# A two-layer transformer block on one core: layer 1's threshold flag a section earlier, transposed chunks in pairs, the output share split over ScalarE and GpSimd, and 128-row row scores in layer 0

## Chip, cores, metric

One NeuronCore of a Trainium2 chip. The time is device microseconds of the whole program for one launch; lower is better. Everything is in one kernel: two layers, each with attention and a feed-forward part.

## What is computed

```python
x = L0_attn_x                                   # (2, 1024, 128) float32
xn = layernorm(x)
x = x + attn0(xn) + moe(xn)                     # attn0: 16 heads of 8, causal softmax; moe: 8 experts, top 2
xn = layernorm(x)
x = x + attn1(xn) + trees(xn)                   # trees: 8 binary trees of depth 7
# attn1: 16 query heads of 64 over 4 key/value heads, rotary positions
scores = where(future, -1e30, q @ k.T / 8)      # 1024 x 1024 for each batch and head
threshold = top_k(scores, 64)[-1]               # the 64th largest of each row
weights = softmax(where(scores < threshold, -1e30, scores))
out = (weights @ v) @ Wo.T
```

## The kernel before

The program runs stage after stage: projections, attention of layer 0, experts, projections of layer 1, trees, attention of layer 1. Each stage writes one instruction list for each engine by hand; semaphores join them. The change touches the two attention stages. B x H heads make 32 in each layer; a sequence of 1024 is 8 row tiles of 128 (`TB = 8`).

**Layer 0** (`attend_layer0`, tensors `a0_`; the profile prints them as `a_`). A section of the loop `heads` works on head n and on the rows of head n+1. TensorE scores head n+1 row by row in 12 units of up to 512 columns (`row_unit`, L350, and for a diagonal tile the mask, L353), VectorE takes each unit's maxima (`peaks`, L463) and from them makes the shift of each row. The queries and keys for this use are 64 partitions (`SHIFT0`) high. The shift is turned (L394) and copied by ScalarE into partitions 64 to 66 of `q` (L439). Then the scores are made again, column by column over 128 partitions (L407, mask L410), so that the shift comes out of the same product; ScalarE exponentiates them (L445), and the product with v follows in three parts `pv` (L374, 32 columns of the array). ScalarE copies the result out (L451) after the sixth column tile; TensorE turns it back (L424); `keep` on VectorE divides. `rows_ahead` puts the row units between the column tiles: 2, then 2, 1, 2, 1, 1, 1, 1, 1. GpSimd only copies v (L331), once in a section.

**Layer 1** (`attend_layer1`). A section n of the loop `sections` has four heads in work: VectorE copies the scores of head n+1 out of PSUM (`keep_scores`, L1463, eight row tiles); ScalarE counts for head n how many scores lie above a trial value (`count`, L1332, eight tiles, three rounds c = 0, 1, 2; VectorE's `first_move` and `second_move`, L1526 to L1581, make the next trial from each round); VectorE sorts head n-1: `tally` (L1421) and `split_tally` read the three rounds, `mark` (L1436) keeps what lies below the value found, `sort` takes 8 + 8 largest in three passes (L1448, L1450, L1452), and the tail to L1693 makes threshold and verdict. Tiles 7 and 6 (1024 and 896 columns) are marked by GpSimd with a compare and a multiply (L1307, L1312, number `EARLY = 2`). Head n-2 is finished: TensorE sums the verdict over the partitions (L1260), VectorE reads that flag (`flags`, L1470), loads it to a register and branches (`judge`: an exact search in the rare bad case), `cut_off` (L1502) writes the cutoffs, ScalarE makes the gates `short` (`gate`, L1342), TensorE turns scores and gates together (`turn`, L1224 and L1226, up to 4 tiles in a chunk, 12 chunks), ScalarE exponentiates a chunk (`weights`, L1351), and TensorE multiplies it with v (`weigh`, L1237). `turn` of chunk x+2 stands behind `weigh` of chunk x. Head n-3 leaves: `copy_out` (L1358), `project` (L1249, eight products of 129 columns, the last of them the softmax sum), and on VectorE `shares` (L1510, the reciprocal) and `leave` (L1519, `x += projected * rec`, from PSUM).

All lists are in program order. TensorE begins a section with the flag of head n-2:

```python
pe.wait_ge(verdict_ready, n - 1)
wait(pe, t_read, (n - 2) * TU)
pe.matmul(ps_flag, g.ones[:, 0:1], verdict[:, :], start=True, stop=True).then_inc(flag_back, 1)
```

ScalarE's section is: counts of round 0, gates of tiles 7 to 4, round 1 with `weights` 0 to 3 between the counts, gates 3 to 0 and `weights` 4, round 2 with `weights` 5 to 8, `weights` 9 to 11. VectorE's is: tally, flag, the first two score copies, judge and cutoff, shares and six sums into x, then marks, score copies and sorting passes, with the steps of the two moves between them.

## Time and profile before

| | |
|---|---|
| median of 3 runs | 2691.27 us (2687.34 to 2691.73) |
| the profiled execution | 2691.92 us, its span 2689.9 us |
| TensorE busy | 2060.2 us, 77% of the span |
| VectorE busy | 1710.9 us, 64% |
| ScalarE busy | 1415.4 us, 53% |
| GpSimd busy | 393.6 us, 15% |
| layer 0's attention | about 110 to 545 us of the span |
| layer 1's attention | about 1210 us to the end |

Busy shares are means over stages with different limits, and a busy TensorE is not one at its peak, since its rows overlap. In a row of the timeline stand the start, the duration and, in brackets, the idle time of that engine before it with what ended it. Neighbouring rows of VectorE and ScalarE overlap by some 0.1 us. Where the kernel repeats a section, one of them is enough: from a section's first row to the next one's.

### The profile page before, as it was taken

What the parts mean: (1) busy time and instruction counts of PE and PEld (TensorE: products, weight loads), DVE (VectorE), ACT (ScalarE), POOL (GpSimd) and SP (SyncE); (2) the same over time, 40 slices, a digit from 0 to 9 for tenths busy, and PEclk for the clock granted to TensorE, in tenths of its full rate; (3) what the DMA queues carried; (4) which work ended last, traced back from release to release, by engine and by line L of the source; (5) the groups of instructions that cost most, each with busy time, mean ns of one, the idle gap of its engine ahead of it and who ended that gap; (6) DMA issues with size and microseconds to landing.
All of it is one profiled execution on the core that took longest, in us unless ns stands there. A gap on an engine that the chain in (4) does not pass through costs nothing. (4 is left out here: it accounts for less than half of the span.)

```text
span 2689.9 us, 36464 instructions
## 1 busy us (share of the span) xinstructions
PE 2060.2 (77%) x10416; PEld 1158.8 (43%) x10448; DVE 1710.9 (64%) x4622; ACT 1415.4 (53%) x2979; POOL 393.6 (15%) x262
## 2 busy tenths in 40 slices
PE   6799999899988968885676777777767567767766
PEld 4233333377764435552343444444434334434434
DVE  4556656521125666765886777777777777877784
ACT  2344444444324213324766666666666566766673
POOL 0000000000012400001212121222212212221211
PEclk7699999999968969997788878788888778888877
DMA  6000000000011200001000000000000000000000
GB/s 179 18 16 15 15 15 15 8 28 1 0 39 55 88 15 0 0 5 44 21 13 25 13 25 12 25 12 24 14 24 17 20 12 18 19 24 12 17 5 21
DMA packets 38267, 62.43 MB, mean 23 GB/s; under 512 B 10226, under 2 KB 15348, under 8 KB 38005
## 3 DMA queue, kind: packets, MB, share of 16 engines
q1 hardware_dynamic: 38069, 60.51, 7.7%
q14 instruction: 161, 1.31, 0.2%
q8 instruction: 37, 0.61, 0.1%
HBM read 34.14 MB, written 17.83 MB: 19 GB/s over the span
## 5 line engine op out<-in xcount | busy, mean ns | idle before, releaser
L1332 ACT ACTIVATE a_trash<-a_sc,a_search 128x1024 bf16<-128x1024 f32 (+7 forms) x768 | 585.7, 766 | 294.2 <-DVE a_search L1581 164.4
L1237 PE MATMUL a_ps_o<-a_kT,a_v 128*65 128x512 f32 (+3 forms) x768 | 376.8, 584 | 214.8 <-ACT a_kT L1351 213.6
L1208 PE MATMUL a_ps_s<-a_k,a_q 128*128 128x512 f32 (+3 forms) x768 | 343.5, 562 | 141.5 <-DVE a_sc L1463 128.1
L1307 POOL TENSOR_SCALAR a_below<-a_sc,a_found 128x1024 f32<-128x1024 f32 x64 | 171.9, 2686 | 1103.5 <-POOLq L1303 1103.5
L1224 PE MATMUL a_ps_t<-g_ident,a_sc 128*128 128x128 f32 x1152 | 298.2, 331 | 33.4 <-ACT a_short L1342 33.3
L463 DVE TENSOR_REDUCE a_top<-a_ps_row 128x1 f32<-128x512 f32 (+3 forms) x384 | 207.4, 557 | 161.4 <-PE a_ps_row L353 107.6
L1226 PE MATMUL a_ps_t<-a_minus,a_short 128*128 128x128 bf16 x1152 | 268.0, 253 | 0.0
L1224 PEld LDWEIGHTS a_ps_t<-g_ident,a_sc 128*128 128x128 f32 x1152 | 199.2, 173 | 154.9 <-issue 92.0
L1351 ACT ACTIVATE a_kT<-a_ps_t 128x512 f32<-128x512 f32 (+3 forms) x384 | 184.6, 481 | 118.8 <-PE a_ps_t L1226 115.0
L1208 PEld LDWEIGHTS a_ps_s<-a_k,a_q 128*128 128x128 f32 x768 | 142.2, 214 | 235.9 <-DVE a_sc L1463 140.5
L445 ACT ACTIVATE a_prob<-a_ps_col 128x1024 f32<-128x1024 f32 (+7 forms) x256 | 158.3, 653 | 147.2 <-PE a_ps_col L407 113.0
L1342 ACT ACTIVATE a_short<-a_sc,a_cutoff 128x1024 bf16<-128x1024 f32 (+7 forms) x256 | 177.0, 764 | 95.3 <-DVE a_cutoff L1502 95.1
L1463 DVE TENSOR_SCALAR_CACHE_REDUCE a_sc<-a_ps_s,g_search 128x1024 f32<-128x1024 f32 (+7 forms) x256 | 207.2, 809 | 24.6 <-PE a_ps_s L1210 9.0
L1237 PEld LDWEIGHTS a_ps_o<-a_kT,a_v 128*65 128x65 f32 x768 | 88.7, 158 | 285.6 <-ACT a_kT L1351 238.0
L1448 DVE MAX8 a_sorted<-a_below 128x8 f32<-128x768 f32 (+7 forms) x256 | 192.8, 754 | 1.2
L1452 DVE MAX8 a_sorted<-a_below 128x8 f32<-128x768 f32 (+7 forms) x256 | 192.5, 752 | 0.0
L1450 DVE MATCH_REPLACE8 a_below<-a_sorted,a_below 128x768 f32<-128x768 f32 (+7 forms) x256 | 189.5, 742 | 0.0
L1226 PEld LDWEIGHTS a_ps_t<-a_minus,a_short 128*128 128x128 bf16 x1152 | 139.8, 121 | 91.6 <-issue 91.5
L584 ACT ACTIVATE ex_hid<-ex_ps_h,le_b 128x512 f32<-128x512 f32 x128 | 87.8, 687 | 128.5 <-PE ex_ps_h L561 128.1
L1332 ACT ACTIVATION_READ_ACCUMULATOR a_trash<-a_sc,a_search 128x1 f32 x768 | 147.0, 191 | 0.0
L350 PE MATMUL a_ps_row<-a_k,a_q 64*128 64x512 bf16 (+3 forms) x384 | 132.5, 346 | 13.9 <-DMA a_k<-stack 12.7
L1312 POOL TENSOR_TENSOR a_below<-a_sc,a_below 128x1024 f32<-128x1024 f32 x64 | 142.4, 2225 | 2.8
(244 smaller groups left out, 3218.3 us busy)
## 6 DMA issues: line engine op xcount, KB each, us to landing
a_v<-g_v SPq DMA_DIRECT2D x32, 260.0 KB, 2.3
q1turned<-p_full SPq DMA_DIRECT2D x32, 256.0 KB, 2.0
a_q<-q1turned SPq DMA_DIRECT2D x32, 256.0 KB, 3.6
a_k<-k1turned SPq DMA_DIRECT2D x32, 256.0 KB, 4.1
stack<-p_parts SPq DMA_DIRECT2D x24, 256.0 KB, 3.8
a_q<-stack SPq DMA_DIRECT2D x32, 96.0 KB, 2.2
a_k<-stack SPq DMA_DIRECT2D x32, 96.0 KB, 2.2
le_w<-d_w SPq DMA_DIRECT2D x1, 2048.0 KB, 8.9
```

The lines of the kernel that those rows point to most:

```text
L463: m = dve.tensor_reduce(top[:, i, c:c + 1], ps_row[:, u % 2, 0:width], AX.X, ALU.max)
L1208: pe.matmul(ps_s[:, j % 2, c:c + w], q[:, p, i * P:width], k[:, p, c:c + w], start=True, stop=True)
L1224: pe.matmul(out, columns(h, i)[:, c * P:(c + 1) * P], g.ident[:, :], is_transpose=True, start=True, stop=False)
L1226: m = pe.matmul(out, short[:, OFF[i] + c * P:OFF[i] + (c + 1) * P], minus[:, :], start=False, stop=True)
L1237: m = pe.matmul(ps_o[0:VW1, lo // HALF, (lo % HALF) * P:CH], v[:, p, c, :], kT[:, x % 2, 0:(hi - lo) * P], start=(c == 0), stop=(c == hi - 1))
L1332: act.activation(trash[:, u % 2, 0:(i + 1) * P], columns(h, i), ACT.Sign, scale=-1.0, bias=trials[:, p, c, i:i + 1], accum_out=balance[:, ...
L1342: act.activation(short[:, OFF[i]:OFF[i] + (i + 1) * P], columns(h, i), ACT.Relu, scale=-STEEP, bias=cutoff[:, h % 2, i:i + 1]).then_inc(ga ...
L1351: act.activation(kT[:, x % 2, 0:w], ps_t[:, x % 2, 0:w], ACT.Exp).then_inc(t_read, 1)
L1448: m = dve.max(sorted_[:, i, 0:8], buf)
L1450: m = dve.match_replace(buf, sorted_[:, i, 0:8], buf, -3.0e38)
L1452: m = dve.max(sorted_[:, i, 8:16], buf)
L1463: dve.tensor_scalar(columns(h + 1, i), ps_s[:, j % 2, 0:(i + 1) * P], shift.rearrange("p n i -> p (n i)"), None, ALU.subtract, ALU.max, ac ...
```

## The change

Layer 0: the row scores use all 128 partitions of `q` and `k`. Partitions 64 to 66 of `q` must then be zero, so GpSimd clears them (`clear`, a sum of two zero tiles) once the head that used them is done, and TensorE waits on `cleared` before a head's first row unit. The row units go 2, 2, 2, 2, 2, 2 between the column tiles. Layer 1: `EARLY` is 3, so GpSimd marks tile 5 too; 12 chunks become 9, each of four tiles; the flag's matmul moves from the head of a section to the chunk loop of the section before, ahead of the last `weigh`; VectorE's list gets a new order; VectorE keeps only the reciprocals of a leaving head, ScalarE scales the eight projected tiles into `share`, and GpSimd adds them to `x` in three pieces. Output transfers wait for those sums.

```diff
-                pool.wait_ge(blank, 3)
+                def clear(n, h):
+
+                    pool.wait_ge(v_ready, n + 2)
+                    pool.wait_ge(col_ready, n * CU + CU)
+                    pool.tensor_tensor(q[SHIFT0:SHIFT0 + NSH, h, :], none[SHIFT0:SHIFT0 + NSH, :],
+                                       none[SHIFT0:SHIFT0 + NSH, :], ALU.add).then_inc(cleared, 1)
+                    pool.wait_ge(cleared, n + 1)
+
+                pool.wait_ge(blank, 4)
                 values(0, 0, True)
                 values(1, 1, True)
-                with pool.Fori(1, NH // 2) as i:
-                    values(i * 2, 0)
-                    values(i * 2 + 1, 1)
+                clear(0, 0)
+                values(2, 0)
+                clear(1, 1)
+                values(3, 1)
+                with pool.Fori(1, NH // NQ) as i:
+                    for h in range(NQ):
+                        clear(i * NQ + (h - 2), (h + 2) % NQ)
+                        values(i * NQ + h, h % 2)
...
                     if u == 0:
                         pe.wait_ge(qk_in[h], i4 * 32 + 32)
+                        wait(pe, cleared, i4 * NQ + (h - NQ + 1))
                     wait(pe, row_read, unit - 1)
-                    last = pe.matmul(ps_row[:, u % 2, 0:width], q[0:SHIFT0, h, i * P:(i + 1) * P],
-                                     k[0:SHIFT0, h, c * CH:c * CH + width], start=True, stop=True)
+                    last = pe.matmul(ps_row[:, u % 2, 0:width], q[:, h, i * P:(i + 1) * P],
+                                     k[:, h, c * CH:c * CH + width], start=True, stop=True)
...
-                        rows_ahead(2 if j in (0, 2) else 1)
+                        rows_ahead(2)
```

Layer 1, the constants, TensorE's loop, GpSimd and ScalarE:

```diff
-        EARLY = 2
+        EARLY = 3
...
-        CHUNKS = [(c, max(c, lo), lo + HALF) for lo in (HALF, 0) for c in range(lo + HALF)]
+        CHUNKS = ([((0, 0, 4),), ((1, 1, 4), (3, 3, 4))] + [((c, HALF, TB),) for c in range(5)]
+                  + [((5, 5, 8), (7, 7, 8)), ((6, 6, 8), (2, 2, 4))])
+        NARROW = 2
+        LAST = (2, 6)
+        GATES = [0, 1, 2, 3, 7, 6, 5, 4]
...
-                def turn(n, h, x):
-
-                    c, lo, hi = CHUNKS[x]
+                def turn(n, h, u, x):
+
                     if x == 0:
                         pe.wait_ge(gated, n * TB + HALF)
-                    if x == EARLY_CHUNKS:
+                    if x == NARROW:
                         pe.wait_ge(gated, n * TB + TB)
...
-                    if gating:
-                        pe.wait_ge(verdict_ready, n - 1)
-                        wait(pe, t_read, (n - 2) * TU)
-                        pe.matmul(ps_flag, g.ones[:, 0:1], verdict[:, :], start=True, stop=True).then_inc(flag_back, 1)
...
+                    odd = h % 2
                     if gating:
-                        turn(n - 2, h + 2, 0)
-                        turn(n - 2, h + 2, 1)
+                        turn(n - 2, h + 2, odd, 0)
+                        turn(n - 2, h + 2, odd + 1, 1)
                     for x in range(TU):
+                        if sorting and x == TU - 1:
+                            pe.wait_ge(verdict_ready, n)
+                            pe.matmul(ps_t[0:1, 1 - odd, 0:TB + 1], g.ones[:, 0:1], verdict[:, :], start=True,
+                                      stop=True).then_inc(flag_back, 1)
                         if gating:
-                            weigh(n - 2, i4 * 2 + h // 2 - 1, h % 2, x)
+                            weigh(n - 2, i4 * 2 + h // 2 - 1, h % 2, odd + x, x)
                             if x + 2 < TU:
-                                turn(n - 2, h + 2, x + 2)
-                        if ahead and x < HALF:
-                            scores(n + 1, i2, p1, HALF + x)
-                        if late and x in (9, 11):
-                            scores(n + 2, i4 * 2 + (h + 2) // 2, 1 - p1, x // 2 - 4)
+                                turn(n - 2, h + 2, odd + x, x + 2)
+                        if ahead and x in (0, 1, 3, 5):
+                            scores(n + 1, i2, p1, HALF + (x + 1) // 2)
+                        if late and x in (6, 7):
+                            scores(n + 2, i4 * 2 + (h + 2) // 2, 1 - p1, x - 6)
...
+                def add(n, x):
+                    lo, hi = ((0, 3), (3, 6), (6, 8))[x]
+                    out = g.x.rearrange("p (b t) d -> p b (t d)", b=B)
+                    xs = out[:, bass.ds(n // H1, 1), lo * P:hi * P].rearrange("p b d -> p (b d)")
+                    pool.wait_ge(shared, n * TB + hi)
+                    pool.tensor_tensor(xs, xs, share[:, lo * P:hi * P], ALU.add).then_inc(added, 1)
...
+                def leave(n, x):
+
+                    lo, hi = ((0, 3), (3, 6), (6, 8))[x]
+                    act.wait_ge(rec_ready, n * 3 + (x + 1))
+                    for t in range(lo, hi):
+                        if t == 0:
+                            wait(act, added, n * 3)
+                        bank, a = PROJ[t]
+                        act.activation(share[:, t * P:(t + 1) * P], projected[bank][:, a, 0:P], ACT.Copy,
+                                       scale=rec[:, t:t + 1]).then_inc(shared, 1)
...
+                    odd = h % 2
                     for s in range(TB):
                         if counting:
                             count(n, h, 0, s)
-                        if leaving and s == 1:
+                        if leaving and s == 2:
                             copy_out(n - 3)
+                    if leaving:
+                        leave(n - 3, 0)
+                        leave(n - 3, 1)
                     if gating:
                         for j in range(HALF):
+                            gate(n - 2, h + 2, j)
+                    if leaving:
+                        leave(n - 3, 2)
+                    if gating:
+                        for j in range(HALF, TB):
                             gate(n - 2, h + 2, j)
                     for s in range(TB):
                         if counting:
                             count(n, h, 1, s)
                         if gating and s % 2:
-                            weights(n - 2, s // 2)
+                            weights(n - 2, odd + s // 2, s // 2)
                     if gating:
-                        for j in range(HALF, TB):
-                            gate(n - 2, h + 2, j)
-                        weights(n - 2, HALF)
+                        weights(n - 2, odd + HALF, HALF)
                     for s in range(TB):
                         if counting:
                             count(n, h, 2, s)
                         if gating and s % 2:
-                            weights(n - 2, HALF + 1 + s // 2)
-                    if gating:
-                        for x in range(2 * HALF + 1, TU):
-                            weights(n - 2, x)
+                            weights(n - 2, odd + HALF + 1 + s // 2, HALF + 1 + s // 2)
```

VectorE (what follows `shares(2)` is the same kind of work in another order; `mark(5)` and `leave` are gone):

```diff
-                        after(did(dve.reciprocal(rec[:, lo:hi], projected[PROJ[lo][0]][:, 0:hi - lo, P])))
-
-                    def leave(x):
-
-                        lo, hi = ((0, 3), (3, 6), (6, 8))[x]
-                        out = g.x.rearrange("p (b t) d -> p b (t d)", b=B)
-                        for t in range(lo, hi):
-                            bank, a = PROJ[t]
-                            xs = out[:, bass.ds((n - 3) // H1, 1), t * P:(t + 1) * P].rearrange("p b d -> p (b d)")
-                            dve.scalar_tensor_tensor(xs, projected[bank][:, a, 0:P], rec[:, t:t + 1], xs, ALU.mult,
-                                                     ALU.add).then_inc(x_kept, 1)
+                        if x == 0:
+                            wait(dve, shared, (n - 3) * TB)
+                        dve.reciprocal(rec[:, lo:hi], projected[PROJ[lo][0]][:, 0:hi - lo, P]).then_inc(rec_ready, 1)
...
                     if sorting:
                         tally()
                         split_tally()
-                    if gating:
-                        flagged = flags()
                     if ahead:
                         keep_scores(0)
                         keep_scores(1)
+                    if sorting:
+                        mark(4)
+                    if gating:
+                        flagged = flags()
+                    if sorting:
+                        mark(3)
                     if gating:
                         judge(flagged)
                         after(made[0])
                         cut_off()
+                    next(first, None)
+                    if sorting:
+                        mark(2)
+                    next(first, None)
                     if leaving:
                         shares(0)
+                    next(first, None)
+                    if leaving:
                         shares(1)
-                        leave(0)
-                        leave(1)
-                    if sorting:
-                        mark(5)
-                    next(first, None)
+                    for _ in first:
+                        pass
                     if ahead:
                         keep_scores(2)
-                    next(first, None)
                     if sorting:
-                        mark(4)
-                    next(first, None)
-                    if sorting:
-                        mark(3)
-                    next(first, None)
-                    if leaving:
-                        shares(2)
-                        leave(2)
-                    if sorting:
-                        mark(2)
-                        sort(5, 0)
                         mark(1)
                         sort(4, 0)
                         mark(0)
-                    for _ in first:
-                        pass
-                    if sorting:
-                        sort(5, 1)
+                        sort(3, 0)
                         sort(4, 1)
+                        sort(3, 1)
+                    if leaving:
+                        shares(2)
                     if ahead:
```

How this moves the instructions is shown at three places. In these rows `a_below` is what is marked and sorted, `a_sc` the scores, `a_rec` the reciprocal, `a_short` the gates; the last number is the columns of what is written.

VectorE at the head of a section, before:

```order
L1430 TENSOR_REDUCE a_found<-a_far 128x8
L1470 TENSOR_SCALAR a_flag<-a_ps_t 1x1
L1463 TENSOR_SCALAR a_sc,a_peak<-a_ps_s,g_search 128x1024
L1463 TENSOR_SCALAR a_sc,a_peak<-a_ps_s,g_search 128x896
L1490 TENSOR_LOAD a_flag
L1490 ISA x2
L1491 COMPARE_AND_BRANCH
```

and now, from the same instruction:

```order
L1479 TENSOR_REDUCE a_found<-a_far 128x8
L1512 TENSOR_SCALAR a_sc,a_peak<-a_ps_s,g_search 128x1024
L1512 TENSOR_SCALAR a_sc,a_peak<-a_ps_s,g_search 128x896
L1485 SCALAR_TENSOR_TENSOR a_below<-a_sc,a_found 128x640
L1519 TENSOR_SCALAR a_flag<-a_ps_t 1x1
L1485 SCALAR_TENSOR_TENSOR a_below<-a_sc,a_found 128x512
L1539 TENSOR_LOAD a_flag
L1539 ISA x2
L1540 COMPARE_AND_BRANCH
```

The flag is read after both score copies and one mark, another mark stands ahead of its load, and the branch follows.

VectorE from the cutoff on, before:

```order
L1502 SCALAR_TENSOR_TENSOR a_cutoff<-a_thr,a_ceiling 128x8
L1510 RECIPROCAL a_rec<-a_ps_o 128x3 x2
L1519 SCALAR_TENSOR_TENSOR g_x<-a_ps_o,a_rec,g_x 128x128 x6
L1436 SCALAR_TENSOR_TENSOR a_below<-a_sc,a_found 128x768
L1526 TENSOR_TENSOR a_reach<-a_wide_aim,a_balance 128x8
L1463 TENSOR_SCALAR a_sc,a_peak<-a_ps_s,g_search 128x768
L1542 RECIPROCAL a_fac<-a_reach 128x8
L1436 SCALAR_TENSOR_TENSOR a_below<-a_sc,a_found 128x640
L1545 TENSOR_TENSOR a_fac<-a_fac,a_search 128x8
L1436 SCALAR_TENSOR_TENSOR a_below<-a_sc,a_found 128x512
L1548 SCALAR_TENSOR_TENSOR a_search<-a_fac,a_search 128x8
L1510 RECIPROCAL a_rec<-a_ps_o 128x2
```

and now, from the first trial's last step to the third reciprocal, which stands eight rows further down:

```order
L1594 TENSOR_TENSOR a_gap<-a_search 128x8
L1512 TENSOR_SCALAR a_sc,a_peak<-a_ps_s,g_search 128x768
L1485 SCALAR_TENSOR_TENSOR a_below<-a_sc,a_found 128x256
L1497 MAX a_sorted<-a_below 128x8
L1485 SCALAR_TENSOR_TENSOR a_below<-a_sc,a_found 128x128
L1497 MAX a_sorted<-a_below 128x8
L1499 MATCH_REPLACE a_below<-a_sorted,a_below 128x640
L1499 MATCH_REPLACE a_below<-a_sorted,a_below 128x512
L1561 RECIPROCAL a_rec<-a_ps_o 128x2
```

Between cutoff and third reciprocal stand now the marks of tiles 2, 1 and 0 and four sorting passes; the sums into `x` are gone.

ScalarE from the end of round 0 on, before:

```order
L1332 ACTIVATE a_trash,a_balance<-a_sc,a_search 128x128
L1342 ACTIVATE a_short<-a_sc,a_cutoff 128x1024
L1342 ACTIVATE a_short<-a_sc,a_cutoff 128x896
L1342 ACTIVATE a_short<-a_sc,a_cutoff 128x768
L1342 ACTIVATE a_short<-a_sc,a_cutoff 128x640
L1332 ACTIVATE a_trash,a_balance<-a_sc,a_search 128x1024
L1332 ACTIVATE a_trash,a_balance<-a_sc,a_search 128x896
L1351 ACTIVATE a_kT<-a_ps_t 128x512
```

and now:

```order
L1368 ACTIVATE a_trash,a_balance<-a_sc,a_search 128x128
L1402 ACTIVATE a_share<-a_ps_o,a_rec 128x128 x6
L1378 ACTIVATE a_short<-a_sc,a_cutoff 128x128
L1378 ACTIVATE a_short<-a_sc,a_cutoff 128x256
L1378 ACTIVATE a_short<-a_sc,a_cutoff 128x384
L1378 ACTIVATE a_short<-a_sc,a_cutoff 128x512
L1402 ACTIVATE a_share<-a_ps_o,a_rec 128x128 x2
L1378 ACTIVATE a_short<-a_sc,a_cutoff 128x1024
L1378 ACTIVATE a_short<-a_sc,a_cutoff 128x896
L1378 ACTIVATE a_short<-a_sc,a_cutoff 128x768
L1378 ACTIVATE a_short<-a_sc,a_cutoff 128x640
L1368 ACTIVATE a_trash,a_balance<-a_sc,a_search 128x1024
```

All eight gates stand ahead of round 1, and two groups of `a_share` stand ahead of them and between them.

## Rows read from the trace of the kernel before

**Rows 1.** Busy time by stretch: span, PE, PEld, DVE, ACT, POOL, PEclk, DMA, GB/s.

```profile
130.00:534.00 404.00, 364.53 (x2437) 145.90 (x2459) 235.08 (x607) 199.80 (x297) 7.32 (x29) 0.99 0.05 13
...
1367.00:2075.00 708.00, 503.39 (x2334) 292.08 (x2333) 535.15 (x1566) 479.37 (x1119) 158.29 (x80) 0.84 0.07 19
```

**Rows 2.** Waits in sixteen sections of layer 1, 1367 to 2075 us: sum, times, longest.

```profile
DVE a_flag L1470 <- PE a_ps_t L1260: 90.6, 16, 7.3
...
DVE a_cutoff L1502 <- issue: 38.5, 16, 2.6
...
ACT a_trash L1332 <- DVE a_search L1581: 84.1, 16, 5.5
...
DVE a_above L1421 <- remote: 9.0, 3, 3.1
```

**Rows 3.** The instructions of L1421 between 1360 and 2080 us.

```profile
L1421 DVE TENSOR_TENSOR a_above<-a_wide,a_balance x17: 182/184/184, 1367.4 to 2078.8; 128x24 f32<-128x24 f32 x17
```

**Rows 4.** Timeline of TensorE in layer 0: start, duration, engine, line.

```profile
308.50 0.22 PE L407 MATMUL a_ps_col<-a_q,a_k 128*128 128x128 bf16 x1
308.65 0.28 PE L350 MATMUL a_ps_row<-a_k,a_q 64*128 64x256 bf16 x1
308.86 0.23 PE L353 MATMUL a_ps_row<-g_maskq,g_identb 128*128 128x128 bf16 x1
308.93 0.38 PE L407 MATMUL a_ps_col<-a_q,a_k 128*128 128x512 bf16 x1
```

**Rows 5.** Timeline of layer 0: TensorE, ScalarE, GpSimd, one section's end.

```profile
300.99 0.61 PE L394 MATMUL a_ps_col<-g_identb,a_shift 128*3 128x128 bf16 x8 [0.48 <-DVE a_shift L472]
...
312.68 1.37 PE L424 MATMUL a_ps_row<-g_ident,a_oT 128*128 128x128 f32 x8
...
311.40 1.02 ACT L451 ACTIVATE a_oT<-a_ps_out 128x1024 f32<-128x1024 f32 x1
...
310.88 0.25 POOL L331 COPY a_v<-l_v 128x72 f32 x1 [13.29 <-PE a_ps_out L374]
```

**Rows 6.** Timeline of VectorE and GpSimd at the head of a section of layer 1.

```profile
1723.41 0.18 DVE L1421 TENSOR_TENSOR a_above<-a_wide,a_balance 128x24 f32<-128x24 f32 x1 [2.96 <-remote]
...
1730.67 1.15 DVE L1463 TENSOR_SCALAR_CACHE_REDUCE a_sc<-a_ps_s,g_search 128x896 f32<-128x896 f32 x1 [0.27 <-DVE a_sc L1463]
...
1734.26 0.36 DVE L1502 SCALAR_TENSOR_TENSOR a_cutoff<-a_thr,a_ceiling 128x8 f32<-128x8 f32 x1 [2.43 <-issue]
...
1727.57 2.36 POOL L1312 TENSOR_TENSOR a_below<-a_sc,a_below 128x1024 f32<-128x1024 f32 x1
```

**Rows 7.** Timeline of GpSimd and VectorE where both read SBUF, an early section.

```profile
1297.07 2.08 POOL L1312 TENSOR_TENSOR a_below<-a_sc,a_below 128x896 f32<-128x896 f32 x1
...
1297.48 2.34 DVE L1436 SCALAR_TENSOR_TENSOR a_below<-a_sc,a_found 128x640 f32<-128x640 f32 x1
...
1260.76 2.51 POOL L1307 TENSOR_SCALAR a_below<-a_sc,a_found 128x896 f32<-128x896 f32 x1
...
1261.77 0.83 DVE L1436 SCALAR_TENSOR_TENSOR a_below<-a_sc,a_found 128x640 f32<-128x640 f32 x1
```

**Rows 8.** Timeline of ScalarE in layer 1: gates, and round 1 of the counts.

```profile
1734.74 3.62 ACT L1342 ACTIVATE a_short<-a_sc,a_cutoff 128x1024 bf16<-128x1024 f32 x4
...
1741.00 1.15 ACT L1332 ACTIVATE a_trash<-a_sc,a_search 128x1024 bf16<-128x1024 f32 x1 [2.64 <-DVE a_search L1548]
...
1748.42 0.20 ACT L1332 ACTIVATION_READ_ACCUMULATOR a_trash<-a_sc,a_search 128x1 f32 x1
```

**Rows 9.** Timeline of VectorE in layer 1: second move, first and last row.

```profile
1708.72 0.17 DVE L1526 TENSOR_TENSOR a_reach<-a_wide_aim,a_balance 128x8 f32<-128x8 f32 x1
...
1712.66 0.16 DVE L1581 SCALAR_TENSOR_TENSOR a_search<-a_fac,a_search 128x8 f32<-128x8 f32 x1
```

**Rows 10.** Timeline of TensorE in layer 1: one product with v, and a later one.

```profile
1743.80 1.97 PE L1237 MATMUL a_ps_o<-a_kT,a_v 128*65 128x512 f32 x2 [2.50 <-ACT a_kT L1351]
...
1750.33 1.02 PE L1237 MATMUL a_ps_o<-a_kT,a_v 128*65 128x512 f32 x2
```

101 lines of the change are left out of this document (54 added, 47 removed).

## The prediction

> **What bounds the kernel now.** I read the busy table by stretch first, then the waits of layer 1, then one section of each attention stage on every engine it uses. The span is 2689.9 us and the execution 2691.9, so 2.0 us lie around the span; the median of the runs, 2691.27, is 0.6 below this execution. The sum is made against 2691.9.
>
> Layer 0: TensorE is busy for 364.5 of 404 us at a granted clock of 0.99, that is at 2.4 GHz, and no other engine for more than 235 [rows 1]. It bounds that stage. A section lasts 13.54 us: GpSimd's copy of v, once in a section, was idle for 13.29 and ran for 0.25 [rows 5].
>
> Layer 1: nothing is full; in 708 us TensorE is busy for 503, VectorE for 535, ScalarE for 479 [rows 1]. Seventeen starts of L1421 lie from 1367.4 to 2078.8, so a section lasts 711.4 / 16 = 44.46 us [rows 3]. VectorE works without a gap except at a section's head: it waits 90.6 / 16 = 5.7 us for the flag and 38.5 / 16 = 2.4 us for the jump over the exact search. ScalarE waits 84.1 / 16 = 5.3 us for the second move [rows 2]. So VectorE's list, with 8 us of holes in it, sets the length, and ScalarE's last counts end just in time. The question for layer 1 is which chain is longest once the holes are filled.
>
> **The change in layer 0.** A product of 128 rows and 128 columns hands over to the mask's in 0.06 us or so: the 128-column mask to the next column product took 308.93 - 308.86 = 0.07. But the 128-row product of 128 columns at 308.50 took until 308.65 before the 64-row one began, 0.15, and that one took 0.21 for its 256 columns before the 128-row mask [rows 4]. At 0.07 for 128 columns they would take 0.07 and 0.12. Every change between 64 and 128 rows costs about 0.09 to 0.1 us. With 12 units in and out that is 24 changes, 2.3 us of a section. The Trainium skill, TensorEngine Tiling (Array Packing), speaks on both sides. Its Overview recommends a smaller tile for a contraction of up to 64, for up to twice the speed: by that the change could only lose; but a single tile is in use here at a time, and a 512-column product takes its columns' time at either height. Its Key Properties say that a change of tiling mode drains the engine; by that, the trace agrees.
>
> Not all of it reaches the end. TensorE waits at the head for ScalarE's copy of the shift, which the first two row units used to cover: 0.4 back. Three more row units now stand ahead of the last `pv` part (2+2+2+2+2+2 against 2+2+1+2+1+1 up to there), about 0.25 each, 0.75 back. So `pv` ends 2.3 x 9/12 less 0.4 and 0.75, only about 0.6 sooner counted from L394; the three units that used to fill TensorE's wait for the output copy are gone from there. L394 began at 300.99, the copy ended at 311.40 + 1.02 = 312.42 and the turns L424 followed at 312.68 for 1.37 [rows 5]: now the turns begin about 0.8 sooner, at 10.9 instead of 11.7, and since the rows are read earlier the 0.48 wait for the shift before L394 goes too. That is 1.25 a section; a stall on the two row buffers may take 0.15. I take 1.1 x 31 = 34 us. Bounds: 0.5 x 31 = 15 if VectorE's maxima hold the pairs up, 2.3 x 31 = 71 if no copy shows. GpSimd's clears lie two sections ahead of their use and cost nothing; without that lead TensorE would wait some 2.4 us for each, the time of its 1024-column product [rows 6].
>
> **The change in layer 1.** I follow one section from L1421 = 0, by the old section from 1723.41 on.
> - Head of VectorE. Tally and two score copies end at about 4.0 (keep_scores(1) was 1.15 [rows 6]), mark(4) at 4.75 (0.83 less overlap [rows 7]). The flag is there by then: verdict, matmul and return need about 3. The 5.7 us hole is gone. The jump stays: from keep_scores(1) to the cutoff were 1734.26 - 1730.67 = 3.6 us, and in it the sequencer, not the engine, is held; so the cutoff comes 3.6 after the flag at 4.85, at 8.4 instead of 10.85.
> - GpSimd in the way. An early section shows a mark of 640 columns that took 2.34 instead of 0.83 us: it began 0.41 after GpSimd's multiply and ended 0.67 after it, so it was held for 1.5 us. A mark of 640 beside GpSimd's compare ran in 0.83 [rows 7]. So a VectorE instruction with two SBUF inputs waits for the rest of a multiply, not of a compare. In the old section the marks came after GpSimd was done; now they stand inside its work, which EARLY = 3 lengthens. GpSimd began its multiply of 1024 at 1727.57, 4.2 in the section's time, for 2.36 [rows 6]. It now starts behind mark(4), 4.75 to 7.1; compare 896 (2.51) to 9.7; multiply 896 (2.08) to 11.8; compare and multiply of 768, by the same slope 2.2 and 1.8, to 14.0 and 15.9. Mark(3) is held until 7.1, hidden under the jump. The reciprocals 0 and 1 and `fac` come at about 9.7: held 2.0. Mark(0) at 14.7: held 1.2. With the passes between them (some 3,500 columns at 0.83 for 640, less overlap, 4.3 us) the third reciprocal is ready at 18.6; without the holds at 15.4.
> - ScalarE. Its `leave(2)` waits for that reciprocal, in front of four large gates and of round 1. Two scaled copies of 128 columns: 0.6, unknown, bounded by 0.3 and 0.8. Gates 3.6 [rows 8], so round 1 starts at 22.8. It takes 1748.62 - 1741.00 = 7.6 us [rows 8]: 30.4. In the old section it began at 17.6.
> - Second move: 1712.66 - 1708.72 = 3.9 before [rows 9], with shorter passes in it now 3.6: 34.1. VectorE is ahead and waits here, about 2.5 us.
> - Round 2 is like round 1, since all chunks are now 512 wide: 7.6, to 41.8. The next tally waits for it. VectorE's remaining passes end near 40.4.
> - TensorE's late score tiles stand behind `keep_scores(6)` and `(7)` and come about 0.4 late for the next head: 42.2. The loop's jump, 9.0 / 3 = 3.0 us in every fourth section [rows 2], was part of 44.46; VectorE now has 1.4 of slack for it, so it adds 0.4 on average: 42.6.
>
> So 44.46 - 42.6 = 1.9 us a section. Of the removed work (sums into x, 1.7 us or so for six, mark(5) 0.9) and the holes, over 8 us, most goes to a chain that runs through ScalarE. Over 29 full sections: 54 us. The first and last sections, where some parts are missing, and the end, where ScalarE and GpSimd replace one VectorE step by three, I leave at nothing, plus or minus 4. Fewer chunks save ScalarE nothing to speak of, since the elements are the same. **Sum:** 2691.9 - 34 - 54 = 2604.
>
> **Rivals.**
> (1) The holds do not happen, because GpSimd's multiplies fall between VectorE's two-input instructions. The reciprocal comes 3.2 sooner: 29 x 3.2 = 93 us less, 2511. For it: only two holds are counted. Against: both are longer than the gaps.
> (2) TensorE's chunk chain eats the gain. After a wait of 2.50 us a pair of products took 1.97 us, six us later 1.02, that is at 1.2 and at 2.4 GHz [rows 10]; now TensorE stands still for some 7 us before round 1. If `weights(4)` or the weights in round 2 come 1.9 late, layer 1 gains nothing: 2658.
> (3) Slower: the same mechanism in full. If TensorE stays at 1.2 GHz from the first product to the last, `weights(4)` ends 3.2 us late in front of round 2, and the chain through `weights(7)` ends the section at 48.7: 29 x 4.2 = 123 more, less 34: 2781. It decides from a section of 44.46 + 34/29 = 45.6 on.
> (4) GpSimd's compares hold VectorE too. Then the cutoff waits 1.2 for compare 896 and a mark up to 2.2 for compare 768: section 46.0, 2691.9 + 45 - 34 = 2703. The mark that ran in 0.83 beside a compare speaks against it [rows 7]. The Trainium skill, SBUF — State Buffer, Who interferes with whom, states it this way: a VectorE instruction with two SBUF inputs contends with any GpSimd instruction that reads SBUF. By that rule the time would be this 2703; the trace agrees for the multiply and not for the compare [rows 7].
> (5) The price of 64 rows is not the change of height, and the row units cost what they did: only 54 gained, 2638.
>
> **How the numbers follow.** Chances: forecast 0.45; (1) 0.20; (2) 0.20; (3) 0.05; (4) 0.04; (5) 0.06. A difference under 0.2%, 5 us, can't be told from none. The forecast, (1), (2) and (5) are faster, 0.91; the slower cases make 0.09, of which their near edges give 0.02 to "same". The range reaches from (1) to beyond (2): 2505 to 2668. Its own spreads leave about 8 in 10 inside.
>
> **What would show it.** Right: layer 0's copies of v about 12.4 us apart and no gap beyond 0.1 us between row unit and mask; no wait before the flag's read; two-input rows of VectorE of 1 to 2 us beside multiplies of GpSimd; ScalarE waiting before the third `a_share` group and starting round 1 near 23; VectorE waiting for round 1. Wrong: a section of L1421 to L1421 outside 41.5 to 43.7, VectorE never waiting for ScalarE, or a clock in layer 1 clearly off 0.84.

## The result, and the profile after

The changed kernel takes 2878.44 us, the median of 4 runs (2874.84 to 2879.5), against 2691.45 us for the kernel before, measured beside it. The ratio is 1.0696, with a 95% interval of 1.0678 to 1.0715. I forecast 2604, in a range of 2505 to 2668. The side is wrong, and the time lies 210 us above the range.

The engines first. The busy table by stretch for the kernel after gives layer 0, then about fourteen sections of layer 1 (columns as in [rows 1]):

```profile
130.00:496.00 366.00, 296.77 (x2314) 130.06 (x2316) 221.82 (x582) 188.83 (x277) 58.89 (x55) 1.00 0.05 14
...
1300.00:2010.00 710.00, 446.66 (x1996) 255.80 (x1995) 490.55 (x1218) 435.72 (x1036) 242.41 (x140) 0.74 0.06 17
```

In layer 1 every engine but GpSimd is less busy than in [rows 1]: VectorE 490.6 of 710 us against 535.2 of 708. No engine has become the bound; they wait for each other. The granted clock is 0.74 instead of 0.84; TensorE also stands still more of the time.

The first instruction of a section (L1421 before, L1470 now) over layer 1 of the kernel after:

```profile
L1470 DVE TENSOR_TENSOR a_above<-a_wide,a_balance x29: 182/184/185, 1305.1 to 2769.2; 128x24 f32<-128x24 f32 x29
```

That is 1464.1 / 28 = 52.3 us a section; one of them, 75.7 us long, holds the exact search, as one of 67.5 us does in the kernel before. An ordinary section is 51.27, and one with the loop's jump 54.2. Over all 32 starts layer 1 took 1366.4 us before and 1578.5 now, 212.1 more. Layer 0's copies of v are 13.18 us apart instead of 13.54, and layer 1 starts 26.1 us sooner. 212 - 26 = 186 of the 187 us are there: layer 1 alone is what has to be explained.

The waits of layer 1 in the kernel after, 1300 to 2800 us (in us: sum, times, longest):

```profile
DVE a_sc L1512 <- PE a_ps_s L1230: 329.6, 60, 7.4
PE a_ps_o L1261 <- ACT a_kT L1385: 318.8, 57, 9.1
...
ACT a_share L1402 <- DVE a_rec L1561: 272.4, 60, 30.3
...
ACT a_trash L1368 <- DVE a_search L1622: 120.0, 29, 4.4
...
DVE a_cutoff L1551 <- issue: 54.3, 22, 4.1
```

The first row has no counterpart in the same view of the kernel before. VectorE's copy of scores out of PSUM waits for TensorE's mask product 60 times, 329.6 / 29 = 11.4 us in a section. The wait for the flag, 5.7 us a section in [rows 2], is gone from the list.

One section on three engines, starting with L1470 at 1820.64. VectorE (start, duration; in brackets its idle time before):

```profile
1824.74 3.10 DVE L1485 SCALAR_TENSOR_TENSOR a_below<-a_sc,a_found 128x640 f32<-128x640 f32 x1
...
1831.53 0.87 DVE L1551 SCALAR_TENSOR_TENSOR a_cutoff<-a_thr,a_ceiling 128x8 f32<-128x8 f32 x1 [2.27 <-issue]
...
1839.82 0.17 DVE L1561 RECIPROCAL a_rec<-a_ps_o 128x2 f32<-128x2 f32 x1
...
1852.18 0.75 DVE L1512 TENSOR_SCALAR_CACHE_REDUCE a_sc<-a_ps_s,g_search 128x512 f32<-128x512 f32 x1 [7.20 <-PE a_ps_s L1230]
...
1860.61 0.15 DVE L1622 SCALAR_TENSOR_TENSOR a_search<-a_fac,a_search 128x8 f32<-128x8 f32 x1
...
1867.73 0.35 DVE L1512 TENSOR_SCALAR_CACHE_REDUCE a_sc<-a_ps_s,g_search 128x128 f32<-128x128 f32 x1 [4.53 <-PE a_ps_s L1230]
```

TensorE in the same section:

```profile
1846.84 1.97 PE L1261 MATMUL a_ps_o<-a_kT,a_v 128*65 128x512 f32 x2 [6.41 <-ACT a_kT L1385]
1851.70 0.31 PE L1230 MATMUL a_ps_s<-a_maskq,g_identb 128*128 128x128 bf16 x1
...
1863.67 1.97 PE L1261 MATMUL a_ps_o<-a_kT,a_v 128*65 128x512 f32 x2 [4.09 <-ACT a_kT L1385]
1867.24 0.31 PE L1230 MATMUL a_ps_s<-a_maskq,g_identb 128*128 128x128 bf16 x1
```

ScalarE in the same section:

```profile
1834.03 1.66 ACT L1402 ACTIVATE a_share<-a_ps_o,a_rec 128x128 f32<-128x128 f32 x6 [5.75 <-DVE a_rec L1561]
...
1840.02 0.62 ACT L1402 ACTIVATE a_share<-a_ps_o,a_rec 128x128 f32<-128x128 f32 x2 [2.54 <-DVE a_rec L1561]
1840.54 3.62 ACT L1378 ACTIVATE a_short<-a_sc,a_cutoff 128x1024 bf16<-128x1024 f32 x4
1844.05 1.14 ACT L1368 ACTIVATE a_trash<-a_sc,a_search 128x1024 bf16<-128x1024 f32 x1
...
1860.87 1.15 ACT L1368 ACTIVATE a_trash<-a_sc,a_search 128x1024 bf16<-128x1024 f32 x1 [4.28 <-DVE a_search L1622]
```

The three views read as one chain. ScalarE waits for VectorE's third reciprocal, starts round 1 at 1844.05 (23.4 into the section), and makes the first `weights` inside it. TensorE has stood 6.4 us for that, runs `weigh(0)` and the next turns, and only then scores tile 4, whose mask is at 1851.70. VectorE, out of work since 1844.98, copies it at 1852.18. Everything behind it on VectorE is late, the second move among it, so round 2 starts at 1860.87 (40.2). There the same happens again: `weigh(5)` needs a `weights` of round 2, tile 7 stands behind `weigh(5)`, and VectorE waits 4.53 us for tile 7 and then has its tail to do.

So the theory for the tests is **A**: score tiles 4 and 7 stand in TensorE's list behind products that wait for ScalarE, whose rounds wait for VectorE, and these two loops of waits make the section long. The rival **B**: VectorE's stalls beside GpSimd, ScalarE's longer list and TensorE's lower clock make it long, and the waits for score tiles are only where it shows.

### The profile page after: what moved, and what is told of

Its sections match the earlier page's. It is cut to its first block, busy times and chain, and to the rows that moved or that the text cites. A ratio compares the mean times of both kernels' runs of the same rounds, so it can differ in the third digit from the quotient of the medians.

```text
span 2876.7 us, 36532 instructions
## 1 busy us (share of the span) xinstructions
PE 2019.7 (70%) x10448; PEld 1154.7 (40%) x10448; DVE 1758.3 (61%) x4335; ACT 1468.8 (51%) x3139; POOL 687.5 (24%) x452
## 4 chain that ended last, share of the span: by engine, by line
DVE 22%; PE 13%; issue 11%; ACT 10%; DVEq 1%; SPq 0%; ACTq 0%; DMA 0%; POOL 0%; POOLq 0%
ACT a_short L1378 5%; PE a_ps_o L1261 5%; DVE a_below L1485 5%; DVE a_sc L1512 4%; DVE a_below L1499 3%; PE a_ps_t L1245 3%; ACT a_trash L1368 3%; PE a_ps_s L1228 3%; DVE a_sorted L1497 2%; PE a_ps_t L1247 2%; DVE a_sorted L1501 1%; ACT a_kT L1385 1%; ACT a_share L1402 1%; DVE a_reach L1567 0%; DVE a_fac L1586 0%
## 5 line engine op out<-in xcount | busy, mean ns | idle before, releaser
L1340 POOL TENSOR_SCALAR a_below<-a_sc,a_found 128x1024 f32<-128x1024 f32 (+2 forms) x96 | 258.4, 2691 | 1004.4 <-POOLq L1336 1004.4
L1385 ACT ACTIVATE a_kT<-a_ps_t 128x512 f32<-128x512 f32 x288 | 168.7, 587 | 166.5 <-PE a_ps_t L1247 166.5
L479 DVE TENSOR_REDUCE a_top<-a_ps_row 128x1 f32<-128x512 f32 (+3 forms) x384 | 196.3, 553 | 93.8 <-PE a_ps_row L366 60.3
L1274 PE MATMUL a_ps_o<-a_wo,a_oT 65*128 (+1 forms) x512 | 93.9, 337 | 202.4 <-ACT a_share L1402 196.7
L1402 ACT ACTIVATE a_share<-a_ps_o,a_rec 128x128 f32<-128x128 f32 x256 | 73.5, 370 | 282.0 <-DVE a_rec L1561 282.0
L1485 DVE SCALAR_TENSOR_TENSOR a_below<-a_sc,a_found 128x640 f32<-128x640 f32 (+4 forms) x160 | 206.9, 1295 | 0.1
L1345 POOL TENSOR_TENSOR a_below<-a_sc,a_below 128x1024 f32<-128x1024 f32 (+2 forms) x96 | 203.3, 2118 | 5.5
L1497 DVE MAX8 a_sorted<-a_below 128x8 f32<-128x640 f32 (+7 forms) x256 | 192.9, 753 | 3.3
L1501 DVE MAX8 a_sorted<-a_below 128x8 f32<-128x640 f32 (+7 forms) x256 | 192.2, 751 | 0.0
L1499 DVE MATCH_REPLACE8 a_below<-a_sorted,a_below 128x640 f32<-128x640 f32 (+7 forms) x256 | 189.4, 741 | 0.0
L1378 ACT ACTIVATE a_short<-a_sc,a_cutoff 128x128 bf16<-128x128 f32 (+7 forms) x256 | 177.5, 782 | 2.5 <-DVE a_cutoff L1551 2.5
```

Of the source, the lines that this page charges most:

```text
L1340: pool.tensor_scalar(lows(i), columns(h - 1, i), found[:, i:i + 1], None, ALU.is_le).then_inc(kinds, 1)
L1378: act.activation(short[:, OFF[i]:OFF[i] + (i + 1) * P], columns(h, i), ACT.Relu, scale=-STEEP, bias=cutoff[:, h % 2, i:i + 1]).then_inc(ga ...
L1485: lane[i] = did(dve.scalar_tensor_tensor(lows(i), columns(hs, i), found[:, i:i + 1], columns(hs, i), ALU.is_le, ALU.mult))
L1497: m = dve.max(sorted_[:, i, 0:8], buf)
L1499: m = dve.match_replace(buf, sorted_[:, i, 0:8], buf, -3.0e38)
L1501: m = dve.max(sorted_[:, i, 8:16], buf)
```

## The experiments

All ratios are to the kernel before, which had medians of 2691.5, 2688.6, 2686.9 and 2687.7 us in the four sets of runs; differences between runs of two sets carry that spread of up to 5 us. "Both tiles moved" is the base from which I went on.

**1. Layer 0's change alone** (the kernel before, with `attend_layer0` of the changed one).

> The kernel before with layer 0's part of the change alone. Theory A (the stages add up; layer 0 gives only what its trace shows, 13.54 to 13.18 us a section): 31 x 0.36 = 11 us less than before, 2680, and the loss lies wholly in layer 1. Rival: layer 0's part brings the 34 us that were forecast and something behind it takes them back: 2657, with the stages behind it unchanged.

Measured: 2670.13 us, ratio 0.9935 [0.9914, 0.9957]. Layer 0's change helps, by 18.5 us against the 2688.6 of the kernel before beside it, of the 34 that I gave it. It is not what makes the kernel slower. It is 10 us more than theory A allowed: beside the 0.36 us in each of 29 sections (10 us), the first interval between two copies of v fell from 40.7 to 35.4 us, and two intervals of 15.07 us became 13.18. Why these were longer before is not shown.

**2. Layer 0 with 128 rows, but the row units in their old places.**

```diff
-                        rows_ahead(2)
+                        rows_ahead(2 if j in (0, 2) else 1)
```

> As l0_only, but the row units stay where they were (2, then 2, 1, 2, 1, 1, 1, 1, 1). Theory A (the height change saves 2.3 us of TensorE's time a section, and the pairs give most of it back: TensorE waits for VectorE's two row buffers and has nothing left to do while ScalarE copies the output): section 11.6 to 12.0, 1.6 to 1.9 less than before, 2632 to 2642. Rival (the height saves no more than 0.4 a section on the path, wherever the units stand): 2680, like l0_only.

Measured: 2679.49 us, ratio 0.9976 [0.9965, 0.9987]. Theory A of that run fell: I took the new placement for a loss, and at 128 rows it is a gain of 9 us. The rival named the right time, 2680, with a reason that does not hold, since the places do matter. TensorE's timeline shows a second, later wait:

```profile
304.51 1.19 PE L440 MATMUL a_ps_row<-g_ident,a_oT 128*128 128x128 f32 x8 [0.25 <-ACT a_oT L467]
306.79 0.61 PE L410 MATMUL a_ps_col<-g_identb,a_shift 128*3 128x128 bf16 x8 [1.10 <-DVE a_shift L488]
308.50 0.61 PE L423 MATMUL a_ps_col<-a_q,a_k 128*128 128x512 bf16 x1 [0.72 <-ACT a_q L455]
...
310.54 1.70 PE L390 MATMUL a_ps_out<-a_prob,a_v 128*32 128x512 f32 x8
```

With the last unit late, VectorE's maxima and the shift are late, and the turn of the shift waits 1.10 us. Behind these gaps a 512-column column product takes 0.61 instead of 0.39 us and eight `pv` products 1.70 instead of 1.05: the granted clock is 1.00 up to 308 us, 0.61 from 308 to 310, 0.59 up to 312.3 and 1.00 again behind it, so TensorE runs at 1.2 GHz for about 4 us. Some sections take 14.60 us and the others 13.02. The pairs keep all sections at 13.18.

**3. The new placement alone, at 64 rows.** The same line as in 2 turned round, in the kernel before.

> The kernel before with only the row units' new places (2, 2, 2, 2, 2, 2), still 64 rows high. Theory A: the pairs' stalls without the saving, about 0.7 to 1.0 us a section more, 2712 to 2722. Rival (places do not matter): 2691.

Measured: 2695.12 us, ratio 1.003 [1.0018, 1.0041]; sections of 14.00 us instead of 13.54. Both theories miss: at 64 rows the placement costs 0.46 a section, less than the 0.7 to 1.0 that I expected: it is worth something only together with the 128 rows.

**4. Score tiles 4 and 7 moved in TensorE's list**, nothing else touched in the changed kernel.

```diff
+                    if ahead:
+                        scores(n + 1, i2, p1, HALF)
                     for x in range(TU):
...
-                        if ahead and x in (0, 1, 3, 5):
-                            scores(n + 1, i2, p1, HALF + (x + 1) // 2)
+                        if ahead and x in (1, 3, 4):
+                            scores(n + 1, i2, p1, HALF + {1: 1, 3: 2, 4: 3}[x])
```

> The changed kernel with two score tiles earlier in TensorE's list: tile 4 of head n+1 ahead of the chunk loop instead of behind the first product with v, tile 7 after product 4 instead of 5. Theory A (VectorE waits 7.2 and 4.5 us a section for these two tiles, which stand behind products that wait for ScalarE): section 52.0 to 43.7, 2878 - 30 x 8.3 = 2630, with 2610 to 2660 allowed. Rival B (the port held by GpSimd and ScalarE's longer list set the section, and the waits move elsewhere): 2850 or more.

Measured: 2646.63 us, ratio 0.9852 [0.9829, 0.9875]. The same work, with two of eight tiles moved, is 232 us faster, and faster than before; the time lies inside theory A's range. The waits of the run in layer 1, 1300 to 2500 us, for fewer sections than above (27):

```profile
ACT a_share L1404 <- DVE a_rec L1563: 234.7, 54, 29.5
...
DVE a_reach L1569 <- DVEq L1462: 54.4, 27, 2.1
...
DVE a_sc L1514 <- PE a_ps_s L1230: 51.1, 63, 1.2
...
ACT a_trash L1370 <- DVE a_search L1624: 19.3, 27, 1.1
```

The wait for score tiles falls from 11.4 to 51.1 / 27 = 1.9 us a section, ScalarE's for the second move from 4.1 to 0.7. In their place stands 2.0 us before `reach`, VectorE waiting for the end of round 1: the wait that I had forecast. An ordinary section takes 42.54 us. Theory A holds and B falls: GpSimd's work, ScalarE's list and the chunks are untouched, and VectorE's stalls beside GpSimd are still there (the marks of 640, 512, 384 and 256 columns take 6.45 us a section, 6.69 in the changed kernel).

**5. Only tile 4 moved.**

> The changed kernel with score tile 4 moved ahead of the chunk loop in TensorE's list; tile 7 stays behind weigh(5). Theory A (VectorE stands where a score tile is behind a weigh that waits for ScalarE): the 7.2 us stand at the 512-column copy goes, and with it the late second move; what is left is the stand at the 128-column copy. VectorE reaches that copy about 38.7 us into the section, weigh(5) runs at 38.0 to 39.0 and the next turns follow, so it stands about 1.7 us there instead of 4.5: section about 44.2, time about 2696 (2680 to 2715). Adding and subtracting the sums of the wait view instead (only 7.2 less, 4.5 left) would give a section of 44.8 to 45, 2715 or more. Rival B (the places of the score tiles matter only together, since the second stand takes over what the first gives back): section still 48 or more, 2790 or more.

Measured: 2686.18 us, ratio 0.9996 [0.9987, 1.0006]: 192 of the 232 us. Ordinary sections take 44.1 to 44.6 us, and the longest wait for a score tile is 1.8 us. The time lies inside theory A's range and below the 2715 of the subtracted waits. It confirms the chain and not the sum of the waits: tile 7's wait was mostly made by tile 4's.

**6. Only tile 7 moved**, behind `weigh(4)`, whose `weights` stand ahead of round 2.

> The changed kernel with score tile 7 moved behind weigh(4); tile 4 stays inside the chunk loop. Theory A: the 7.2 us stand at the 512-column copy stays, so the second move ends near 40 us and round 2 of ScalarE runs from 40.2 to 47.9; only the 4.5 us stand at the 128-column copy goes, and ScalarE's round 2 bounds the section in its place: section about 48 instead of 51.3, time about 2775 (2755 to 2795). If the waits just added, it would be 2878 - 29 x 4.5 = 2748. Rival B (tile 7 alone is what makes the section long): about 2680.

Measured: 2811.48 us, ratio 1.0467 [1.0448, 1.0486], 67 us less than the changed kernel; I had allowed 2795 at most. VectorE's waits, 1300 to 2500 us:

```profile
DVE a_sc L1512 <- PE a_ps_s L1230: 211.3, 64, 7.2
DVE a_cutoff L1551 <- issue: 63.8, 19, 4.7
DVE a_above L1470 <- ACT a_trash L1368: 25.3, 20, 1.3
```

The 7.2 us wait stays, and the tally now waits for ScalarE's last count, as expected; ordinary sections of 47.88 are there, but about every second one is 49 to 50; where I looked (1794 us), tiles 0 and 1 at the head come 0.8 and 1.1 us late too. The mechanism was right, the size of what remains 1 us a section too small. 192 + 67 is 259, not 232: the two loops share a part.

**7. The flag's matmul back at the head of the section**, both tiles moved.

```diff
-                        if sorting and x == TU - 1:
-                            pe.wait_ge(verdict_ready, n)
-                            pe.matmul(ps_t[0:1, 1 - odd, 0:TB + 1], g.ones[:, 0:1], verdict[:, :], start=True,
-                                      stop=True).then_inc(flag_back, 1)
...
+                    if gating:
+                        pe.wait_ge(verdict_ready, n - 1)
+                        pe.matmul(ps_t[0:1, h % 2, 0:TB + 1], g.ones[:, 0:1], verdict[:, :], start=True,
+                                  stop=True).then_inc(flag_back, 1)
```

> Both score tiles moved as before, but the flag's matmul put back at the head of TensorE's section, one section later than the change has it. In the run with both tiles moved TensorE came to the flag's matmul at 3.3 us of the next section anyway, while VectorE reads the flag at 7.1. Theory A (VectorE's new order, with copies and a mark ahead of the flag, is what took the 5.7 us wait away; where TensorE's matmul stands is worth nothing): no difference from 2646.6, within 6 us. Rival B (the matmul's early place is what does it): the flag's answer comes 1 to 5 us late, section 43.5 or more, time 2675 or more.

Measured: 2650.48 us, ratio 0.9858 [0.9843, 0.9874], against 0.9852 in run 4: the same. VectorE reads the flag at 7.1 us of its section, behind two copies and a mark, and TensorE makes the product at 4.2 us even from the head of its own section; in the kernel before it made it at 5.0 to 7.9 us in most sections, and VectorE was ready for it at 1.0. So the later read covers most of the 5.7 us, and the rest of the change brings the product forward too; the new order by itself was not run. The part that the change's title speaks of first, the matmul a section earlier, is worth nothing here.

**8. The output share back on VectorE**, both tiles moved: reciprocals and eight sums into `x` on VectorE, as in the kernel before; `leave` on ScalarE and `add` on GpSimd gone.

```diff
+                            dve.scalar_tensor_tensor(xs, projected[bank][:, a, 0:P], rec[:, t:t + 1], xs, ALU.mult,
+                                                     ALU.add).then_inc(shared, 1)
...
-                    if leaving:
-                        leave(n - 3, 0)
-                        leave(n - 3, 1)
```

> Both score tiles moved (as in the run of 2646.6), and the output share put back on VectorE: its eight sums into x straight from PSUM behind the reciprocals, no scaled copies on ScalarE, no additions on GpSimd. Theory A (the split takes 2.2 us of sums off VectorE, but makes ScalarE's gates and round 1 wait for reciprocals: 2.9 and 4.4 us of waits in a section, and VectorE then waits 2.0 us for round 1): without the split ScalarE starts its gates right behind the cutoff, round 1 by about 15 us instead of 23.4, VectorE's waits of 2.0 and 1.2 us shrink or go, its list is 2.2 us longer: section about 42.2 instead of 42.5, time 2637 (2622 to 2652), no loss from undoing the split. Rival B (the split is worth what it takes off VectorE): section 44.7, time about 2710 (2690 or more).

Measured: 2654.08 us, ratio 0.9881 [0.9863, 0.9898], 2 us above the range that I gave it and 7 above run 4; the intervals of the two ratios overlap. B, with 2690 or more, falls: the split over three engines gives about 7 us (19 by the far ends of the intervals). Theory A had the size nearly right and round 1 wrong. Rows of its waits, 1300 to 2500 us:

```profile
ACT a_trash L1367 <- DVE a_search L1624: 173.0, 27, 7.1
...
DVE a_cutoff L1545 <- issue: 92.4, 27, 4.6
...
DVE a_above L1464 <- ACT a_trash L1367: 27.4, 22, 1.3
```

ScalarE no longer waits for reciprocals, but 173.0 / 27 = 6.4 us a section for the second move. In the section from 1916.13 on, round 1 starts at 18.1 us (23.4 in run 4), but VectorE ends its second move at 35.0, hardly before the 35.2 of run 4. ScalarE's round 2 follows, and the next tally waits 1.3 us for it. So an earlier round 1 buys nothing here: VectorE's list up to the second move and round 2 behind it set the section.

**9. The third reciprocal early**, both tiles moved: `shares(2)` directly behind `mark(1)` in VectorE's list.

```diff
                         mark(1)
+                    if leaving:
+                        shares(2)
+                    if sorting:
                         sort(4, 0)
                         mark(0)
                         sort(3, 0)
                         sort(4, 1)
                         sort(3, 1)
-                    if leaving:
-                        shares(2)
```

> Both score tiles moved as before, and VectorE's third reciprocal put right behind mark(1), ahead of four sorting passes and mark(0). In the run with both tiles moved ScalarE waited 4.4 us for that reciprocal at 19.17 us of the section, and VectorE then waited 2.0 us for the counts of round 1 and 1.2 for score tile 6. Theory A (that chain, reciprocal - two scaled copies - four large gates - round 1, sets the end now): the reciprocal comes at about 16.2, round 1 starts 3 us sooner, VectorE's waits of some 3.4 us go, section 42.5 -> 39.5 to 40.2, time 2565 to 2590. Rival B (VectorE's own list sets the end and its waits are slack that only moves): section 42.0 or more, time 2630 or more.

Measured: 2595.01 us, ratio 0.9656 [0.9643, 0.9669], 5 us beyond the range. Ordinary sections take 41.16 us instead of 42.54. ScalarE's second wait for a reciprocal is gone in most sections, but the section fell by 1.4 and not by 2.3 to 3. The mark of 128 columns shows where part went, in the groups by form of VectorE, 1300 to 2500 us (busy us, mean ns):

```profile
L1487 DVE SCALAR_TENSOR_TENSOR a_below<-a_sc,a_found 128x256 f32<-128x256 f32 x29 | 36.3, 1253 | 0.0
...
L1487 DVE SCALAR_TENSOR_TENSOR a_below<-a_sc,a_found 128x128 f32<-128x128 f32 x28 | 28.9, 1032 | 0.0
```

`mark(0)` came forward and now begins together with one of GpSimd's sums into `x`, which hold it: 1.03 us in place of 0.34 in run 4.

**10. Run 9 with `EARLY` at 2**: GpSimd marks two tiles, VectorE marks tile 5 late in its list.

```diff
-        EARLY = 3
+        EARLY = 2
...
                         sort(6, 2)
+                        mark(5)
                         sort(5, 0)
```

> The run of 2595.0 (both score tiles moved, third reciprocal early) with EARLY back at 2: tile 5 (768 columns) is marked by VectorE late in its list, GpSimd's compare and multiply of 768 columns are gone. Theory A (a two-input mark of VectorE is held for the rest of a GpSimd multiply, which cost mark(1) of 256 columns 2.1 us instead of 0.4, while VectorE's list sets the section): 1.7 us of hold go ahead of the second move, 0.95 of mark come back behind it; ScalarE waits 3.1 us for the second move now, so the section falls by 0.8 to 1.7: 39.5 to 40.4, time 2560 (2545 to 2580). Rival B (holds lie on no path, marks do): section 42.1, time about 2620 (2605 or more). Rival C (the reciprocals 0 and 1, not mark(1), start the chain that bounds): no change beyond 5 us from 2595.

Measured: 2567.02 us, ratio 0.9552 [0.9536, 0.9567], the fastest version of this study, 4.5% below the kernel before and 10.8% below the changed one, and inside theory A's range. The same groups by form:

```profile
L1487 DVE SCALAR_TENSOR_TENSOR a_below<-a_sc,a_found 128x768 f32<-128x768 f32 x29 | 29.0, 1001 | 0.0
...
L1487 DVE SCALAR_TENSOR_TENSOR a_below<-a_sc,a_found 128x256 f32<-128x256 f32 x29 | 20.4, 703 | 0.0
...
L1487 DVE SCALAR_TENSOR_TENSOR a_below<-a_sc,a_found 128x128 f32<-128x128 f32 x29 | 11.1, 382 | 0.0
```

VectorE took over a mark of 1.00 us, and the marks of 256 and 128 columns together fell by 1.2. All marks together take 6.91 us a section, with one mark more, and took 7.14 in run 9. GpSimd's third tile had cost VectorE as much in stalls as it took off it, and cost it ahead of the second move, where it counts. Ordinary sections are now 39.4 to 41.4 us.

## Why the prediction was wrong, point by point

**The step that failed** is in the walk through layer 1: "VectorE is ahead and waits here, about 2.5 us", and with it "VectorE's remaining passes end near 40.4". I followed VectorE and ScalarE, and gave TensorE only "late score tiles ... about 0.4 late for the next head". VectorE's passes also wait for score tiles, and the diff that I printed has their new places in TensorE's list: `if ahead and x in (0, 1, 3, 5)`. Tile 4 stood behind `weigh(0)` before too; there round 1 began at 17.6 us, and VectorE came to the tile 2.5 us after its mask, as these rows of the kernel before show (TensorE, then VectorE, in the section of [rows 6]):

```profile
1747.98 0.22 PE L1210 MATMUL a_ps_s<-a_maskq,g_identb 128*128 128x128 bf16 x1
...
1750.49 0.73 DVE L1463 TENSOR_SCALAR_CACHE_REDUCE a_sc<-a_ps_s,g_search 128x512 f32<-128x512 f32 x1
```

I had worked out myself that round 1 would move to 22.8, and that VectorE would be ahead, and did not move `weigh(0)` and tile 4 with it. Tile 7 moved from behind `weigh(3)`, fed in round 1, to behind `weigh(5)`, fed in round 2, one round later. Run 4 shows both steps: with the two tiles out of the way the wait before `reach` is 2.0 us, where I had said 2.5, and an ordinary section takes 42.54, where I had 42.2.

**What held, and what of it is luck.** In the section above, by the walk's own steps: the flag's wait is gone; round 1 started at 23.4 (22.8) and ended at 31.0 (30.4); the third reciprocal came at 19.2 (18.6). These three steps were within 0.6 us. For the third reciprocal that is partly luck, as two errors cancel. Reciprocals 0 and 1 came at 13.2 and 13.4 and not at 9.7. The way from there to the third took 6.0 us and not 8.9: of the 3.2 us of holds that I had counted on it, 0.6 was there (mark(1), 1.05 instead of 0.47), and mark(0) took its 0.34. Behind these steps VectorE's waits for tiles 4 and 7 add 7.20 and 4.53 us, and an ordinary section takes 51.27.

**What was mis-sized.** Run 4 with its 2646.6 us is still 43 above my 2604. Layer 0 gave 0.36 a section, not 1.1, and 18.5 us in all (run 1), not 34. In layer 1 the forecast was 54 us less; run 4's 32 starts take 1348.8 us against 1366.4, 17.6 less. The loop's jump was to be hidden but for 0.4 on average; every fourth section is 45.85 instead of 42.54, 0.8 on average, and with the score tiles of the head run 4's sections average 43.5 us in the steady part, where I had 42.6. The cutoff of the section above came at 10.9 and not at 8.4: I had mark(4) end at 4.75, ahead of GpSimd's multiply, but it was held until 7.2, the flag is read behind it at 7.1, and the cutoff follows 3.8 later, where I had reckoned 3.6 from the flag on.

**Layer 0.** The price of a change of height held at the product: the product of 256 columns that took 0.21 us to its mask [rows 4] now takes 0.11:

```profile
302.75 0.27 PE L366 MATMUL a_ps_row<-a_k,a_q 128*128 128x256 bf16 x1
302.86 0.22 PE L369 MATMUL a_ps_row<-g_maskq,g_identb 128*128 128x128 bf16 x1
```

And TensorE's busy time fell from 364.5 / 404 x 13.54 = 12.2 us of a section [rows 1] to 296.8 / 366 x 13.18 = 10.7. That is 1.5 of the 2.3 that I had counted. The path did not follow, since 1.2 us of new idle time stand against it. TensorE now has gaps of 0.70 us before the turns, 0.72 for the copy of the shift into `q`, twice 0.30 for a row buffer and 0.42 for an exponential. I had counted 0.4 for the copy and 0.15 for the buffers. Run 3 shows the placement's own cost, at 64 rows, at 0.46 a section.

**The rivals.** (1) is refuted: mean marks of 640 columns take 2.99 us in the changed kernel against 0.83 before. (2) and (3), TensorE's clock: after standing still for 6.41 and 4.09 us TensorE is granted 0.50 from 1846.8 to 1851.8 and from 1863.6 to 1867.6, which is 1.2 GHz, and 0.98 between 1851.8 and 1859.4. `weigh(0)` and `weigh(5)` take 1.97 us there, and ScalarE waits 2.04 and 1.71 us for turned chunks. This is inside the loop: it lengthens the waits and does not make them. From `weigh(0)` to the mask of tile 4 TensorE needs 4.9 us; by this trace's rows at 2.4 GHz, each counted from its start to the next one's (0.86 for the pair of products, 0.68 for four turns, 0.86 for the two score products), it would need 2.4. So by this estimate about 2.5 of the 7.2 us is the clock's, and 4.7 would be left without it. In run 4 `weigh(0)` takes the same 1.97, the granted clock of 1300 to 2010 us is 0.80 and not 0.74, and the kernel is fast. (3) had the right side by the wrong mechanism.

(4) was nearer than I gave it. GpSimd's compares do hold a two-input mark, for a short time:

```profile
1824.79 2.37 POOL L1345 TENSOR_TENSOR a_below<-a_sc,a_below 128x1024 f32<-128x1024 f32 x1
1827.12 3.11 POOL L1340 TENSOR_SCALAR a_below<-a_sc,a_found 128x896 f32<-128x896 f32 x1
...
1832.36 2.20 POOL L1340 TENSOR_SCALAR a_below<-a_sc,a_found 128x768 f32<-128x768 f32 x1
...
1832.40 1.26 DVE L1485 SCALAR_TENSOR_TENSOR a_below<-a_sc,a_found 128x384 f32<-128x384 f32 x1
```

Mark(2) began 0.04 us after the compare of 768 columns and took 1.26 us instead of 0.61; the compare kept the 2.20 us that it has in sections where no mark runs beside it. Mark(3), at 1827.83, took 1.42 instead of 0.75. The compare of 896 columns took 3.11 instead of 2.51 us; mark(4), held by the multiply, still ran in its first 0.72 us (1824.74 + 3.10 = 1827.84), and I read the lengthening as that. A mark that began 1.0 us into a compare kept its 0.83 [rows 7]. So a compare holds such a mark by some 0.65 us when the mark begins near the compare's start, and not for the compare's whole length, as a multiply does. The kernel before has such a pair too, which I had not read: a mark of 768 columns at 1294.51, 0.08 us after a compare, took 1.77 us instead of 1.01. The Trainium skill, SBUF — State Buffer, Who interferes with whom, counts any GpSimd instruction that reads SBUF as such a neighbour; these rows agree with it in kind, where [rows 7] alone did not.

(5) holds in part: the price is the height, but the path gained 0.36 of the 1.5 us.

**What stays open.** I did not run the nine chunks of four tiles against the twelve of before, nor VectorE's new order without the other parts, nor GpSimd's third tile on its own in the changed kernel; so how run 4's gain (1 - 0.9852, 40 us) divides is shown only for layer 0 (about 18), the flag's matmul (nothing) and the split (7 at most).
